# Sparse-splat attention and mixture-of-experts layer on one core: the heads in two halves, and the expert steps gathered behind the value products

## The reference, cut to what matters

```
q, k, v = heads(xn @ Wq.T), heads(xn @ Wk.T), heads(xn @ Wv.T)      # 16 heads of 16
scores  = q k / sqrt(16), causal
features of q and of k: 8 Gaussians exp(-0.5 |x-p|^2 / s^2) and 8 tanh(...) per head
gsa     = scores + sensitivity * (features of q) . (features of k)
attn    = (1-b) * softmax(scores) v @ Wo.T + b * softmax(gsa) v @ Wo.T
experts: 2 of 16 per token (sqrt(softplus) gate), at most 128 tokens each:
         silu(xe W1) * (xe W3) @ W2, weighted, plus one shared expert for all tokens
```

## Time and profile before

| | us |
|---|---|
| time, median of 3 runs (lowest, highest) | 377.26 (376.95, 378.29) |
| time of the profiled execution | 378.75 |
| its span | 376.9 |
| PE busy | 334.7 (89%) |
| DVE busy | 230.7 (61%) |
| ACT busy | 194.1 (51%) |
| POOL busy | 65.7 (17%) |
| mean granted clock of PE | 0.947 of full |

### The profile page before, as it was taken

The page is one execution under the profiler, slowest core; times in us unless marked ns, Lnnn a source line. Parts: engine busy times, 40 slices in busy tenths (PEclk is TensorE's granted clock), DMA queues, the critical chain, the costliest instruction groups (busy, mean ns, idle before and its releaser), DMA issues.

```text
span 376.9 us, 6181 instructions
## 1 busy us (share of the span) xinstructions
PE 334.7 (89%) x2172; PEld 174.8 (46%) x2172; DVE 230.7 (61%) x614; ACT 194.1 (51%) x278; POOL 65.7 (17%) x82
## 2 busy tenths in 40 slices
PE   0999996788979999999999999999999999989965
PEld 0643663343345544554455445544554454335433
DVE  4555857587674665567556655766577558776222
ACT  1699824525414365436543654366346547767530
POOL 7200140400047530110111011102010007710000
PEclk9999768598979999999999999999999999999995
DMA  6408623304341354245655565547555525510011
GB/s 220 131 0 103 107 38 41 60 13 60 47 135 15 41 75 73 71 89 102 142 153 105 113 139 153 107 93 154 129 125 111 79 53 127 143 42 2 0 57 56
DMA packets 27330, 33.01 MB, mean 88 GB/s; under 512 B 6593, under 2 KB 20097, under 8 KB 27297
## 3 DMA queue, kind: packets, MB, share of 16 engines
q1 hardware_dynamic: 23745, 28.32, 37.4%
q0 software_dynamic: 2128, 4.22, 3.9%
q10 hardware_dynamic: 1424, 0.04, 0.2%
HBM read 15.60 MB, written 4.28 MB: 53 GB/s over the span
## 4 chain that ended last, share of the span: by engine, by line
PE 72%; DVE 14%; ACT 9%; issue 3%; DMA 1%; SPq 0%; DVEq 0%; ACTq 0%
PE ps L817 16%; PE ps L745 9%; PE ps L800 8%; PE ps L788 7%; PE ps L754 7%; PE ps L718 6%; ACT arena_p L636 6%; DVE mx L1093 5%; PE ps L676 4%; PE ps L773 2%; PE ps L695 2%; PE ps L758 2%; PE ps L791 2%; DMA acc<-in_x_dram 1%; ACT small L641 1%
## 5 line engine op out<-in xcount | busy, mean ns | idle before, releaser
L636 ACT ACTIVATE arena_p<-ps 128x1024 f32<-128x1024 f32 (+1 forms) x192 | 147.2, 811 | 79.4 <-PE ps L800 53.7
L1093 DVE TENSOR_REDUCE mx<-ps 128x1 f32<-128x512 f32 (+3 forms) x160 | 89.3, 590 | 33.2 <-PE ps L718 22.7
L817 PE MATMUL ps<-arena_p,v_full 128*32 128x512 f32 (+3 forms) x768 | 72.6, 496 | 0.6 <-ACT arena_p L636 0.6
L718 PE MATMUL ps<-stage 96*128 96x512 bf16 (+3 forms) x160 | 51.5, 362 | 7.1 <-DVE mx L1093 4.7
L788 PE MATMUL ps<-stage 98*128 98x512 bf16 (+1 forms) x192 | 51.9, 337 | 4.7 <-ACT arena_p L636 4.2
L800 PE MATMUL ps<-stage 98*128 98x512 bf16 (+1 forms) x192 | 47.4, 332 | 3.0 <-ACT arena_p L636 2.4
L641 ACT ACTIVATE small<-ps 128x176 f32<-128x176 f32 x24 | 7.6, 318 | 64.1 <-PE ps L745 64.1
L387 POOL DMA_INDIRECT wt<-xn_scratch,ids_sb x16 | 15.2, 951 | 133.2 <-PE ps L735 127.6
L817 PEld LDWEIGHTS ps<-arena_p,v_full 128*32 128x32 f32 x768 | 20.2, 110 | 35.4 <-issue 30.3
L754 PE MATMUL ps<-arena_o,small 88*128 88x256 f32 x96 | 27.4, 409 | 8.3 <-DVE small L1116 6.3
L788 PEld LDWEIGHTS ps<-stage 98*128 98x128 bf16 x192 | 18.8, 100 | 23.5 <-ACT arena_p L636 9.8
(11 more groups left out here) (193 smaller groups left out, 418.5 us busy)
## 6 DMA issues: line engine op xcount, KB each, us to landing
w_sb<-in_w_dram SPq DMA_DIRECT2D x16, 352.0 KB
stage<-split SPq DMA_DIRECT2D x48, 96.0 KB, 2.9
stage<-split SPq DMA_DIRECT2D x48, 64.0 KB, 2.7
arena_o<-in_w_dram SPq DMA_DIRECT2D x16, 176.0 KB
stage<-split SPq DMA_DIRECT2D x80, 32.0 KB, 2.5
ye_scratch<-wt SPq DMA_DIRECT2D x16, 128.0 KB, 1.8
stage<-split SPq DMA_DIRECT2D x32, 48.0 KB
acc<-in_x_dram SPq DMA_DIRECT2D x2, 512.0 KB, 4.6
```

Source lines behind the costliest of these rows:

```text
L636: A(to, ps[:, 1 + 2 * s:3 + 2 * s, off:CH], ACT.Exp, scale=SCALE).then_inc(done, 1)
L718: ins = M(b[:, 0:n1 - n0], lhs, ks[0:KR, pr, h, n0:n1], start=True, stop=not diag)
L817: ins = M(ps[c:c + 2 * HD, 0, off:CH], v_full[:, jb + s, g * GH + h, :], of, start=jb + s == 0, stop=end)
L1093: V.reduce_max(mx[:, it // TC, h, it % TC, pc:pc + 1], b[:, 0:n1 - n0], AX.X).then_inc(aux_free, 1)
```

## The change

The heads are cut into two halves of eight. The prologue projects, featurises and splits only the first half (`PRO` has 4 `proj` and 4 `feat` instead of 8 and 8); q features and k features of a half are stacked on the 128 partitions. The second half is done in the slots of groups 1 and 2 (`HALF`; slot 24 is the first of group 1). Expert and shared steps stand in slot 0 of a pair, up to four in one slot, from four rows of work; experts in slots 52 to 124, shared rows after them, in slots 120 to 156. Routing is spread over slots 10 to 36. Nine parameter loads become one. Thirds are all on DVE. The branch for large scores is cut in two as well; it is not taken with these inputs. The core of the diff:

```diff
-        PRO += [("proj", (s, m, tc)) for m in range(KD) for s in range(2) for tc in range(NC)] + [("par", 0)]
-        PRO += [("feat", (s, tc, w)) for s in range(2) for tc in range(NC) for w in range(2)]
-        PRO += [("gate", 0)] + [("v", n) for n in range(NT // 2)]
+        PRO += [("proj", (s, tc)) for s in range(2) for tc in range(NC)] + [("par", m) for m in range(2)] + [("gate", 0)]
+        PRO += [("feat", (tc, w)) for tc in range(NC) for w in range(2)] + [("v", n) for n in range(NT // 2)]
...
+        def chain(kinds, count, at):
+            return [(at + 4 * (n + step), (kind, n)) for step in range(3, -1, -1) for n in range(count) for kind in kinds[step:step + 1]]
...
-        LATER = 8
-        first_rest = [(n // 2, ("pre", t)) for n, t in enumerate(max1[LATER:])] + [(4, ("pre", ("shift", 1)))]
-        first_maxima = spread_late(max0, 5, 9) + [(12, ("shift", 0))] + spread_late(max1, 10, 20) + [(22, ("shift", 1))]
+        first_rest = [(n // 3, ("pre", t)) for n, t in enumerate(max1)] + [(6, ("pre", ("shift", 1)))]
+        first_maxima = spread_late(max0, 7, 11) + [(13, ("shift", 0))] + spread_late(max1, 11, 21) + [(22, ("shift", 1))]
+        HALF = [(26, ("proj1", (0, 0))), (27, ("proj1", (0, 1))), (30, ("proj1", (1, 0))), (31, ("proj1", (1, 1))),
+                (30, ("p0", 4)), (34, ("p0", 5)),
+                (34, ("feat1", (0, 0))), (35, ("feat1", (0, 1))), (38, ("feat1", (1, 0))), (39, ("feat1", (1, 1))),
+                (41, ("product", 1)), (42, ("p0", 6)), (43, ("p0", 7)),
+                (42, ("rest", 4)), (43, ("rest", 5)), (44, ("p1", 4)), (45, ("p1", 5)), (46, ("third", 4)), (47, ("third", 5)),
+                (48, ("rest", 6)), (49, ("rest", 7)), (50, ("p1", 6)), (51, ("p1", 7)), (52, ("third", 6)), (53, ("third", 7))]
+        S_ROUTE, S_EXPERT, S_SHARED, S_ADD = (10, 36), 52, 116, 140
+        long += chain(("xT", "gu", "hT", "y"), E, S_EXPERT)
...
+        ROWS_QK = [(n, 2 * n + (1 - 2 * n) * step, h) for step in range(3) for n in range(2) for h in range(GH)]
+        ROWS_F = [(n, 2 * n + (1 - 2 * n) * step, h, w) for step in range(3) for n in range(2) for h in range(GH)
+                  for w in ((0, 1) if n == 0 and step < 2 else (None,))]
...
             for j in range(N_QK):
+                if j % 2 == 0:
+                    wait_parts(sp, j // 2 % 2, j // 4)
                 load_qk_row(sp, 0, 0, j, qk_in[0])
+            for j in range(N_F - 1):
+                if ROWS_F[j][0:3] in ((0, 0, 0), (0, 1, 0), (0, 2, 0)):
+                    for at in (2, 3):
+                        wait_parts(sp, at, ROWS_F[j][1])
+                load_feature_row(sp, 0, 0, j, f_in[0])
+            shift_rows(-1, 0, 0)
+            sp.wait_ge(zeros_out, 16)
+            sp.wait_ge(gaps_ready, 1)
+            load_feature_row(sp, 0, 0, N_F - 1, f_in[0])
             for j in range(N_QK):
                 load_qk_row(sp, 1, 1, j, qk_in[1])
...
-            n_v = PRO.index(("v", 0))
-            for n in range(n_v):
-                prologue(n)
...
+            for n in range(len(PRO)):
+                prologue(n)
...
             pe.wait_ge(qk_in[0], 16 * N_QK)
-            for t in max0:
-                aux(-1, t, 0)
-            prologue(n_v)
-            prologue(n_v + 1)
-            aux(-1, ("shift", 0), 0)
-            prologue(n_v + 2)
-            prologue(n_v + 3)
-            for t in PRE1:
+            for t in PRE0:
                 aux(-1, t, 0)
```

More of the change, by code:

```diff
@@ L241, in bass_splat_attention_moe_layer @@
-        first_maxima = spread_late(max0, 5, 9) + [(12, ("shift", 0))] + spread_late(max1, 10, 20) + [(22, ("shift", 1))]
[L243 to L246, removed]
+            late_slots = [n for n in range(first, last + 1) if n % 4]
@@ L272, in bass_splat_attention_moe_layer @@
         PRE0 = max0 + [("shift", 0)]
-        PRE1 = max1[0:LATER]
         AB = 3
-        UNBANKED = ("add", "route")
+        FIRST_WEIGHTS = ("product", 1)
+        OWN_E = next(e for e in range(E) if AT["xT", e] >= OWN_AT[1] * NSLOT)
+        UNBANKED = ("add", "route", "p0", "p1", "rest", "third", "product")
         CUM = 4
-        sequence = [(-1, t) for t in PRE0 + PRE1]
+        sequence = [(-1, t) for t in PRE0]
         for g in range(NG):
@@ L622, in _ @@
             A(g_[10][:, :, :], g_[11][:, :, :], ACT.Sqrt).then_inc(gate_act, 1)
-            A(TMP, GG, ACT.Exp)
-            for at in range(4, 8):
+            A(PRE_, GG, ACT.Exp)
+            for at in range(4):
                 act.wait_ge(part_done[at], 1)
@@ L646, in _, with proj, features_of @@
             pe.wait_ge(ident_ready, 1)
+            def proj(m, s, tc, b):
+                for k in range(KD):
+                    last = M(b, wt[:, s, k, m * P:(m + 1) * P], xnT[:, k, tc * CH:(tc + 1) * CH],
+                             start=k == 0, stop=k == KD - 1)
+                return last
+            def features_of(m, tc, w, b):
+                cols = slice(tc * CH, (tc + 1) * CH)
+                steps = ((1, qk_half[m]), (0, sq[m])) if w == 0 else ((2, qk_half[m]),)
+                for n, (row, src) in enumerate(steps):
+                    for s in range(2):
+                        side = slice(64 * s, 64 * s + 64)
+                        last = M(b[side, :], gT[:, m, row, side], src[:, s, cols], start=n == 0, stop=n == len(steps) - 1)
+                return last
             def prologue(n):
@@ L900, in _ @@
                             slot(3)
+                if g + 1 == OWN_AT[1]:
+                    with pe.If(needed > 0):
+                        for n in range(AB):
+                            pe.wait_ge(*freed[DONE_BY[g] - 1 - n])
+                        own(1, g % QB, g % 2)
             pv(NG - 1, NP - 1)
@@ L1083, in aux @@
                     return
-                bank, count = place(g, t)
+                if kind in HALVES or kind in ("p0", "p1"):
+                    return
+                if kind in ("rest", "third", "product"):
+                    {"rest": rest_of, "third": third_of, "product": product}[kind](a)
+                    return
+                bank, full, count = place(g, t)
                 b = ps[:, bank, :]
-                dve.wait_ge(aux_full, count)
+                dve.wait_ge(aux_full, full)
                 if kind == "max2":
@@ L1216, in _ @@
                             aux(g, t)
+                if g + 1 == OWN_AT[1]:
+                    with dve.If(needed > 0):
+                        own(1)
             evac(NG - 1, 1)
```

612 lines of the change are left out of this document (292 added, 320 removed).

## The result

The changed kernel takes 387.54 us (median of 4 runs, 383.42 to 388.68), the kernel before, on the same chip, 377.77 (4 runs, 376.95 to 379.42). The ratio is 1.0233, with an interval of 1.0148 to 1.0318: the kernel is slower, but whether by more than 2 per cent stays open. Medians and ranges printed here are over all executions, while ratios, and differences of medians between two kernels, take only those in the faster of two states, which differ in the granted clock. The profiled execution took 388.14, with a span of 386.4 against 376.9, so that 9.5 us have to be found.

What follows compares the result with a forecast made beforehand. PE was taken to bound groups 1 to 6, with some 25 us lost at the start. Terms 1.3 + 5 + 3 + 2 - 3 = +8.3 on the profiled 378.75 gave 387.1, less 1.5 over the median: 385.6 us, range 370 to 397.

Steps and rivals of the forecast that it cites:

- Items 1 to 3: Prologue and group 0: shorter prologue, SP's copies as the path, fewer shared rows; group 0 ends 21.8 us earlier, at 98.1.
- item 1: Prologue, with half the projections and features: features out at 32.5 us, v at 40, last first part at 36.5.
- Item 4: Behind group 0: the moved projections, features and four shared rows add 23.1 us.
- Item 5: Group 1's slot 17 to group 2's slot 5: DVE and ACT have more work than PE, +5 us (0 to 8).
- item 8: Groups 1 to 5: y no longer waits for hT's copy, -3 us (-4 to 0).
- item 7: Expert pairs: the tanh, now between ACT's first and second exponential, delays PE's next scores, +2 us (-1 to +6).
- Item 6: Expert weights, now needed in the next pair, come late: 1 us lost about once a group, +3 us (0 to 20).
- rival A: Groups 1 to 6: moved work fills PE's idle time, 240 us or less there, 372 us in all; chance 0.2.
- B: Whole kernel, no change: the costs and relief behind the start cancel, 377 to 379 us; chance 0.13.
- C: Late weights: gu waits 1 to 2 us in most of 13 experts, +12 us, 398 us; chance 0.1.
- D: Clock: stays at 0.72 in group 0's rest, drops to 0.9 in groups 1 and 2; +5 and +4, 394 us; chance 0.1.

Runs made afterwards that it cites:

- sprelief: Changed kernel with POOL instead of SP issuing group 0's six k feature rows and group 1's 12 q and k rows: 386.39 us, ratio 1.0196.
- noweights: Changed kernel without the loads of expert weights beyond the first three experts, output not that of the layer: 415.32 us, ratio 1.0066.
- spread: Changed kernel with each expert step in a slot of its own in the pair, y first: 421.03 us, ratio 1.0149.
- route: Changed kernel with the routing in slots 1 to 22 instead of 10 to 36: 421.11 us, ratio 1.0245.
- combo_route2: combo2 with the routing in slots 1 to 22 instead of 10 to 36, on the same slower chip: 409.96 us, ratio 0.9873.
- ctl: The changed kernel itself, run again as control on a slower chip: 417.93 us, ratio 1.0149.
- combo2: The kernel of combo again, on a slower chip: 400.20 us, ratio 0.9726.
- combo: Changed kernel with two edits: second-half projections and features in group 0's two shift waits, 18 row loads from SP to POOL: 384.99 us, ratio 1.0169.

## Why the prediction was right

The forecast was 385.6 us, slower by 8.3; measured are 387.5, and 9.8 more than before in the same comparison. Its steps, against the trace of the changed kernel on the first chip:

- **Items 1 to 3, the start.** The last feature product ends at 33.9 (forecast 32.5), the v products at 41.0 (40), the last first part at 37.1 (36.5). First scores at 52.2 (54) and 70.5 (74); the 16 feature rows cost SP 11.8 us, 0.74 each, the 1.04 of the earlier trace rows did not return. The three parts' errors (a later first part, cheaper rows, a slower second chunk) cancel, which is luck: group 1 starts at 97.7 where 98.1 was forecast. The second chunk took 27.3 us, forecast 24. Its clock was higher than assumed (0.91, not 0.87); what the item left out is that PE idles 4.1 us in it. Two sums of item 1 do not come out of their terms as given either: 21.1 + 1.2 + 4.5 + 5.2 is 32.0 and not 32.5, and 32.5 with 1.2, 1.07 and an eviction of 0.7 (L556) is 35.5 and not 36.5. sprelief shows by intervention that SP's list is the path.
- **Item 4, the moved work.** 23.6 us of PE time, some 1.5 of them from group 2's clock, forecast 23.1.
- **Item 5, the second half.** Forecast +5. The wait is where the item put it: 4.4 us of idle in 26 us with DVE at 21.6. Over groups 1 and 2 PE idles 6.5 us against 3.3 before, so **+3.2**, but with the 1.7 us of `y` waits that are gone there (item 8). The waits for exponentials in the two groups rose by 3.0 and those for DVE's maxima by 1.7, so the item alone is **+4.7**. The item reckoned with DVE's excess over PE (20 us against 13.8); the larger part of the waits is for ACT, to which it gave 16.3 us of work. Some of these, late in group 2, may be item 7's.
- **Item 6, the weights.** Forecast +3; the waits for a load are two, 1.3 us together, near the start of group 4 and half-way through it, not once a group. The path is as described. First the issues that stand ahead, then PE's wait:

```profile
240.76 1.05 SPq L529 DMA_DIRECT2D ye_scratch<-wt  x1
241.85 1.62 SPq L517 DMA_DIRECT2D w_sb<-in_w_dram  x1
243.51 0.42 SPq L518 DMA_DIRECT2D arena_o<-in_w_dram  x1
```

```profile
249.45 1.42 PE L777 MATMUL ps<-w_sb,wt 128*128 128x352 f32 x4 [1.14 <-DMA arena_o<-in_w_dram]
```

  From the last issue's start to PE's are 5.9 us, where I took 4.5 for the landing; and SP took 3.1 us for three issues that cost 1.2 in the earlier trace rows. That most pairs had more room than I gave them is what two waits in 13 experts say; no run varied it. What noweights wins (0.8 per cent, 1.5 us by the medians) is near the forecast too, but its control has no wait for a load in its trace, so that it is not shown to be this item.
- **Items 7 and 8, the tanh and the relief.** In groups 3 to 6 the waits for exponentials are 4.9 us against 0.9, so item 7 is **+4.0**, forecast +2. That the place of the tanh is behind them is supported by spread, in which these waits are gone from groups 3 and 4, though the edit moves the other steps too. Of the item's own terms, 0.32 and three times 1.02 are 3.4, and not 3.2. ACT's wait stands where it was foreseen, ahead of the tanh and behind the first exponential:

```profile
196.50 0.32 ACT L656 ACTIVATE small<-ps 128x176 f32<-128x176 f32 x1 [3.00 <-PE ps L777]
196.72 1.94 ACT L651 ACTIVATE arena_p<-ps 128x1024 f32<-128x1024 f32 x2
```

  The waits of `y`, 3.6 us, are gone entirely (item 8, -3). A term had no place in the sum: a maximum of the next group now often stands three steps behind `gu`, needs its bank and waits for the two DVE operations behind the tanh (L747 and L739 for L1151, 2.9 us in seven waits). Where `y` waited before, a maximum waits now.
- **The sum.** Forecast +1.3 + 7 for groups 0 to 6, measured -21.7 + 32.0 = +10.3; the tail gave back 0.8. The mechanism is as forecast, the start wins less than is put behind it, but that the sum is off by only 1.2 us is partly luck: item 6 was 1.7 too high, item 7 2.0 too low, and the 2.9 us of the bank were missing.
- **A slip in the text.** Under "What would show it" groups 1 to 6 were to take 254 us. That does not follow from the items: 215.9 + 23.1 + 7 is 246, the figure that rival A uses. Measured are 249.0, so 254 was wrong and 246 was 3 us low. Two figures of rival A are slips as well: half of 8.7 is 4.4 and not 3.7, and the earlier trace rows give DVE and ACT 66 and 55 per cent and not 63 and 51. Neither changes a chance.
- **The rivals.** A needed 240 us or less in groups 1 to 6 and no more idle time than before; they take 249.0 and PE idles 8.5 us more than before. B falls with the ratio, whose interval lies above 1. C is excluded by noweights. Of D there is a trace, group 2 at 0.96, which is 1.5 us, but group 1 at 1.00 and group 0's second chunk at 0.91, above the 0.87 assumed. The Trainium skill (TensorE: Matmul & The Clock Gate, HAM oscillation) says that the clock is lowered again over a wait for a DMA, so that the products behind it start slow. The 0.71 of the first chunk, behind a wait of 6.6 us, agrees, but that chunk was low before too (0.76 and 0.72 in the earlier trace rows).
- **The signs of being wrong.** None of the three appeared: SP is not idle before either shift, group 0 ends at 97.7 and not before 92, and PE idles 3.6, 2.7, 3.9 and 2.6 us in groups 2 to 5, never less than 1.5.

What the prediction did not see at all is that the start could not have been made much faster: it says of the scatters that they "have until slot 52". They do, with nothing to spare. That made no difference to the change itself, but three kernels that had won 2.4, 4.8 and 10.4 us by the start of group 2 then waited 1.5, 7.0 and 6.8 us for the first gather, and ended within 0.3 per cent of each other.

## What to carry to other kernels

Work moved from a prologue into a full pipeline costs its whole time there (here 23.6 us for 23.1). It pays only by the idle time that its removal closes at the start, and that has to be read off the queue that sets the start (here SP's copies), not off the engine that is idle. Before making a start faster, follow every chain with a due time, here routing, scatters, list, gather: if one is just in time, the lead is lost at it. And moving such a chain forward has its own price, here 2.6 us in route and 5.0 in combo_route2, lost in group 0 before the first scatter. And a comparison holds for its chip: the combination of the two edits was 1.7 per cent slower than the kernel before on one and 2.7 per cent faster on another.

## What the runs showed of the hardware

The kernel before takes 378 us on two of the chips and 410 to 412 on three. The changed kernel's traces on one of each kind are alike up to group 1 (its start 97.7 and 98.2) and in groups 2 to 4, where the second is even faster (38.80 + 44.25 + 44.68 = 127.7 us against 39.87 + 44.51 + 46.37 = 130.8). The second loses 12.2 us in group 1 and 15.5 us from group 5 to the end. In both stretches POOL issues sixteen indirect DMAs, in the first the scatters of the token numbers and in the second the gathers of the results; DVE and ACT stop together, and PE behind them. From the timeline of ctl, one instruction each of DVE, ACT and PE with the wait in front of it, at the gathers (issued from 310.1 to 328.9):

```profile
332.90 0.42 DVE L947 TENSOR_TENSOR acc<-ps,acc 128x256 f32<-128x256 f32 x1 [15.79 <-remote]
333.01 0.32 ACT L656 ACTIVATE small<-ps 128x176 f32<-128x176 f32 x1 [17.16 <-remote]
...
333.65 0.39 PE L832 MATMUL ps<-stage 98*128 98x128 bf16 x2 [13.52 <-ACT arena_p L651]
```

POOL meanwhile issues on, one every 1.25 us. On the first chip the same sixteen gathers stand beside engines that work on. None of the five traces from the two faster chips has a remote wait on DVE or ACT; each of the nine from the slower chips has one of 12 to 17 us at the gathers. The standstill moves with the scatters: in ctl they are issued from 111.4 to 130.6, and DVE stands still for 16.2 us in three pieces, the last up to 134.4; in route they are issued from 93.6 to 112.8, and it stands still for 15.5 us, up to 116.3. In combo2, with scatters from 107.7 to 129.9, the remote waits there are only 0.6 us on DVE and at most 3.9 on ACT, though group 1 still takes 7.4 us more than in combo. So the standstill is not always as long; why is open. What stops the engines is not known: no run took the indirect DMAs away. How the kernel before loses 33 us on such a chip has no trace.
